# Graph network on one core: 48 instead of 32 of 104 edge groups read on TensorE from the table in SBUF

## The reference

```python
norm = deg_inv_sqrt[row] * deg_inv_sqrt[col]
msgs = embedding_weight[row] * norm[:, None]
out = jax.ops.segment_sum(msgs, col, num_segments=n)
```

## Time and profile before

| | |
|---|---|
| median of 3 runs | 5939.31 us (5934.91 to 5939.78) |
| the profiled execution | 5942.14 us, of which the span from first to last instruction is 5940.4 us |
| busy share of the span | PE 82%, PEld 55%, DVE 60%, ACT 30%, POOL 68% |
| convolution pass 1, from its first read to its last add | about 1050 to 1784 us |
| convolution pass 2, from its table to its last add | about 1803 to 2537 us |
| the rest of the span | edge network before, attention layers from 2566 us on |

### The profile page before, as it was taken

One profiled execution on the slowest core, in us unless ns is written; L12 is line 12 of the kernel. 1 busy time (PEld: TensorE's weight loads), 2 busy tenths in 40 slices (PEclk: granted clock), 3 DMA queues, 4 the chain that ended last, 5 costly groups with the idle time before them and its releaser, 6 DMA issues.

```text
span 5940.4 us, 130692 instructions
## 1 busy us (share of the span) xinstructions
PE 4842.8 (82%) x43965; PEld 3280.3 (55%) x43965; DVE 3567.0 (60%) x6811; ACT 1755.2 (30%) x3748; POOL 4068.4 (68%) x4236
## 2 busy tenths in 40 slices
PE   4999998666665666659999996799999958999997
PEld 4777776566665555625555554355555534555554
DVE  6566554666656555546666666466666655666666
ACT  3222222555540000023333331333333223333331
POOL 4777775677776777757777771777777447777771
PEclk8999998778877878879999998899999989999998
DMA  4665654222222222234454542445444324445442
GB/s 112 178 169 163 169 168 124 72 70 67 71 62 70 65 71 66 64 75 120 126 127 127 128 126 61 96 125 130 126 127 127 108 58 119 125 126 131 125 127 64
DMA packets 688913, 648.24 MB, mean 109 GB/s; under 512 B 401395, under 2 KB 483770, under 8 KB 688250
## 3 DMA queue, kind: packets, MB, share of 16 engines
q1 hardware_dynamic: 548266, 463.96, 26.1%
q0 software_dynamic: 135616, 175.22, 15.5%
q10 hardware_dynamic: 4368, 0.70, 0.1%
HBM read 550.21 MB, written 89.17 MB: 108 GB/s over the span
## 4 chain that ended last, share of the span: by engine, by line
PE 49%; issue 18%; POOL 16%; DVE 13%; DVEq 2%; DMA 1%; ACT 1%; SPq 0%; ACTq 0%; POOLq 0%
PE ps L1064 15%; POOL rows L379 11%; PE ps L911 10%; PE ps L1005 7%; POOL rows L392 5%; PE ps L1026 4%; PE ps L1040 2%; DVE region L1668 2%; PE ps L1016 2%; PE ps L938 1%; PE ps L991 1%; DVE acc L1814 1%; DVE region L1646 1%; PE ps L926 1%; DVEq L1620 1%
## 5 line engine op out<-in xcount | busy, mean ns | idle before, releaser
L392 POOL DMA_INDIRECT rows<-table,idx x2340 | 2265.9, 968 | 1017.3 <-issue 706.6
L1064 PE MATMUL ps<-region,hot 128*128 128x272 f32 x4992 | 1297.0, 404 | 134.9 <-DVE acc L1814 123.3
L673 ACT ACTIVATE region<-ps 128x512 f32<-128x512 f32 x1248 | 677.7, 597 | 1640.4 <-PE ps L1005 1640.4
L1064 PEld LDWEIGHTS ps<-region,hot 128*128 128x128 f32 x4992 | 904.9, 191 | 426.0 <-issue 199.4
L1814 DVE TENSOR_TENSOR acc<-acc,ps 128x272 f32 x1248 | 543.5, 436 | 842.7 <-PE ps L1064 727.5
L379 POOL DMA_INDIRECT rows<-table,idx x728 | 700.1, 962 | 262.7 <-issue 221.0
L911 PE MATMUL ps<-hot,region 128*128 128x192 bf16 (+1 forms) x6144 | 743.9, 292 | 23.6 <-issue 22.9
L1789 DVE TENSOR_TENSOR region<-ps,region 128x1056 f32<-128x1056 f32 x582 | 724.5, 1251 | 43.0 <-issue 39.7
L1005 PE MATMUL ps<-xT,wcat 64*128 64x512 f32 x2496 | 711.6, 647 | 12.6 <-ACT region L673 12.6
L911 PEld LDWEIGHTS ps<-hot,region 128*128 128x128 bf16 x6144 | 659.4, 117 | 60.9 <-issue 23.0
L409 POOL DMA_INDIRECT rows<-table,idx x576 | 546.0, 948 | 211.0 <-issue 174.9
(11 more groups left out here) (304 smaller groups left out, 6678.1 us busy)
## 6 DMA issues: line engine op xcount, KB each, us to landing
hot<-hot_dram SPq DMA_DIRECT2D x624, 256.0 KB
turned<-turned_dram SPq DMA_DIRECT2D x624, 128.0 KB
rows<-table,idx POOLq DMA_INDIRECT x3644
hot_dram<-hot SPq DMA_DIRECT2D x104, 512.0 KB
xwin<-table SPq DMA_DIRECT2D x1664, 24.0 KB
region<-hot_dram SPq DMA_DIRECT2D x64, 512.0 KB, 3.7
region<-d_dram SPq DMA_DIRECT2D x104, 256.0 KB
turned_dram<-turned SPq DMA_DIRECT2D x104, 256.0 KB
```

The costliest lines, as they stand in the source:

```text
L392: pool.indirect_dma_start(rows[:, n % 2, j, :], None, table, bass.IndirectOffsetOnAxis(ap=idx[:, s:s + 1], axis=0)).then_inc(rows_in3[n % ...
L673: act.activation(rz[g % 2][:, 2 * t + side, :], ps[:, Z + side, :], ACT.Relu).then_inc(rz_made, 1)
L1064: mm = pe.matmul(ps[:, sum_bank(k, side, i), 0:PC + H], hot[:, b, 4 * side + 2 * i + j, :], px[b][:, 4 * side + 2 * i + j, :], start=(j == ...
```

## The change

The rule that chooses the dense groups is another one. `DENSE` grows from 32 to 48 groups, `PLAIN` shrinks from 72 to 56; `NS` goes from 128 to 192. No other line changes; the code above walks the new lists.

```diff
-DENSE = [g for g in range(G) if 7 * g % 16 >= 11]
-PLAIN = [g for g in range(G) if 7 * g % 16 < 11]
+DENSE = [g for g in range(G) if 6 * g % 13 >= 7]
+PLAIN = [g for g in range(G) if 6 * g % 13 < 7]
 ND, NP, NS = len(DENSE), len(PLAIN), 4 * len(DENSE)
 ITEMS = [x for i in range(NS) for x in [("dense", i)] + [("plain", p) for p in range(NP * i // NS, NP * (i + 1) // NS)]]
```

## The result

The changed kernel takes 5768.1 us (median of 4, 5761.06 to 5775.75), the kernel before on the same chip 5939.55 us (5934.91 to 5950.96): a ratio of 0.971, with a 95% interval from 0.969 to 0.972. The gain is 171 us where 239 were forecast; 5768 lies in the range, 68 us above the number.

The account below looks back on a forecast made before the run. GpSimd's gathers were taken to bound both passes, with the TensorE-VectorE loop taking over: -141.2 us in pass 2 and -116.4 in pass 1, +19 for slow reads, -239 in all, so 5700 us, range 5640 to 5800.

Parts of the forecast that it names:

- The gathers set the pace before, and no longer do after: Both passes: GpSimd's gathers set 10.03 us a plain group; after the change the TensorE-VectorE loop, mean cycle 10.39, becomes the bound.
- the gathers stay the bound: Rival, both passes: if coupling costs nothing, each falls by 161 us, giving 5618; chance 0.12.
- VectorE's wait for plain sums falls from 157 us to under 20: Sign of being right: VectorE's idle time before L1626 for L938 falls from 157 us to under 20.
- The step near 10.8 and 10.4 us: Sign of being right: from one plain sum to the next, near 10.8 us in pass 1, 10.4 in pass 2.
- A cycle is 9.24 or 11.70 us: Loop: one plain group with three or four dense quarters behind it takes 9.24 or 11.70 us, mean 10.29.
- The pause of 1.52 us: TensorE's cycle: 1.52 us left over in which it waits for the first fold, just before the third read.
- Meanwhile TensorE has read the next two quarters: Loop: during VectorE's plain adds TensorE reads two quarters; the third read waits behind the first quarter's sum.
- One third read in ten as slow: Clock term: a tenth of 112 third reads takes 3.88 instead of 2.22 us, 19 us; bounds 0 and 186.
- Slow reads thus follow the waits for rows, and these go: Clock term: reads at 1.2 GHz come behind longer stalls for gathered rows, which vanish; 16 of 17 after short stalls were fast.
- the clock swings: Rival: every third read starts at 1.2 GHz, 186 us come back, gain 72, giving 5867; chance 0.14.
- Stationaries slow the gathers: Rival: VectorE's added L1641 hold GpSimd for their whole length, 32 us a pass, giving 5723; chance 0.05.
- SyncE's loads at nothing: SyncE's 48 x 2 tile loads a pass instead of 32 x 2 arrive in time and cost nothing.

Follow-up runs that it names:

- the first alone: Changed kernel with the sum and add of each dense quarter put two quarters behind its read instead of one: 5747.4 us, ratio 0.967.
- the second alone: Changed kernel with the next dense group's stationaries made in the first three quarters instead of one in each: 5720.0 us, ratio 0.963.
- the mended schedule: Changed kernel with dense sums two quarters behind their reads and the next group's stationaries made in the first three quarters: 5662.1 us, ratio 0.954.

## Why the prediction was right, and where it was off

- *The gathers set the pace before, and no longer do after.* Right: with half of them the kernel before gets 424 us shorter, the changed one stays as it is. They wait for L938 for 91.5 us in 40 places. The rival "the gathers stay the bound" (5618) is out.
- *VectorE's wait for plain sums falls from 157 us to under 20, the clock rises above 0.90, the reads' mean falls.* Right: 1.4 us; 0.92 and 0.91; 261 ns where the page of before has 292. The step near 10.8 and 10.4 us was not met: 11.72 and 11.10.
- *A cycle is 9.24 or 11.70 us.* Right where nothing else comes in: the 16 cycles of pass 2 that hold three quarters and begin behind a group's first or second quarter take 9.34 and 9.37 us on average in the timeline, with no slow read. The pause of 1.52 us is there with 1.4 to 1.7 us.
- *"Meanwhile TensorE has read the next two quarters."* This step failed. In 32 of 110 steps the second read begins a dense group and waits for a stationary that VectorE makes only after the plain adds: 53.9 us of waits. Part of them stands in place of the pause that was forecast; by itself it made these steps some 0.5 us longer, 15 us in all, and 13 of the slow reads come right behind such a wait. The order could be seen in the code (a stationary in each quarter, the read waits for all four). The trace of before has 1.2 us of this wait, since TensorE waited for gathered rows then; with half the gathers the same kernel shows 19.7 us of it in pass 1.
- *"One third read in ten as slow."* This term was mis-sized most: 19 us were forecast, and some 70 came, from 46 slow reads instead of 11. The price was right, 1.65 us where 1.66 was taken. "Slow reads thus follow the waits for rows, and these go" is the step that failed: the waits for rows went, but 45 of the 46 slow reads follow the new loop's own pauses and waits. The forecast took its number from reads behind single stalls of up to 2.55 us, 16 of 17 at full speed; behind the pauses of the new loop, none longer than that, four in ten were slow. So the rival "the clock swings" (5867) held for part of the steps, some 70 of its 186 us. The rule of the Trainium skill that the prediction weighed ("TensorE: Matmul & The Clock Gate", section "A second HAM failure mode: psum-queue depth-cycling") is borne out in part: with brief and frequent pauses 46 of 110 steps had a slow read.
- *Stationaries slow the gathers.* Hardly: a gather's mean is 961 ns, 12 more than before, with 50% more L1641 beside them, and the gathers aren't the bound.
- *SyncE's loads at nothing.* Nearly: L926 waits 1.4 us in pass 2 and 4.8 in pass 1 for `dhot`.

The sum: the passes are 87 us over the forecast without its clock term (5681), some 70 of them slow reads and some 15 the wait for a stationary. That 5768 lies in the range owes something to luck: the range was drawn for the clock alone, with two thirds of the third reads slow at its upper end, and the wait was not in it. The version with early stationaries and filled pauses, all but free of both, measures 5699, with steps of 10.97 and 10.54 where 10.84 and 10.39 were worked out. Of the 18 us that are left, a part is this version's own: its steps that follow a group's last quarter are 0.5 to 0.8 us longer than the others on average, and their first quarter holds L1639 (0.21) and two stationaries instead of one (0.39 more). No run took the rest apart.

## What to carry to other kernels

When the slowest engine is relieved, walk the waits of the loop that takes over through every phase of its period, not through one typical cycle: here the wait that was missed falls on two of seven cycles. Work out what the new pauses do to the clock as a term of its own, with bounds: the slow reads were some 70 of the 87 us. Two waits in a row on one path are better removed together: here taking away the first alone gave 21 us, the second alone 48, both 106. And the balance point between two ways to do a piece of work belongs to the schedule: 44 groups beat 48 by 61 us as the code stood, and 48 with the mended schedule (5662) beat both; 44 with that schedule was not run.

## What the runs showed of the hardware that was not expected

The length of one pause of TensorE does not say at which clock the next read runs: behind 1.71 us a read took 2.23 us, behind 1.72 us another took 3.88. The loop hid nothing of such a read: with 3.88 us instead of 2.23 the step took 11.68 instead of 10.03. Nine tenths of a microsecond of matmuls without use in each pause, some 100 us of TensorE's time in all, went with a granted clock of 1.00 in the two stretches instead of 0.95 and 0.98 (one profiled execution each), and made the kernel 21 us faster.
